# Two float32r parts for the attention scores, laid out on two halves of the partitions, in a macaron transformer block

## What is computed

```python
q = bitnet_linear(hidden_states, q_weight, q_scale)   # 32 heads of 16
k = bitnet_linear(hidden_states, k_weight, k_scale)   # 8 heads of 16
v = bitnet_linear(hidden_states, v_weight, v_scale)
...
scores = jnp.einsum('bhqd,bhkd->bhqk', q, k) / np.sqrt(HEAD_DIM)
attn = jax.nn.softmax(scores, axis=-1)
out = jnp.einsum('bhqk,bhkd->bhqd', attn, v)
```

## Time and profile before

| what | us |
|---|---|
| median of 3 runs | 1261.84 |
| span of the profiled execution, first to last instruction | 1259.9 |
| busy: TensorE matmuls (PE) | 1121.5 |
| busy: VectorE (DVE) | 935.9 |
| busy: ScalarE (ACT) | 715.8 |
| busy: GpSimd (POOL) | 276.3 |

### The profile page before, as it was taken

One profiled execution on the slowest core, in us unless ns is written; L12 is line 12 of the kernel. 1 busy time (PEld: TensorE's weight loads), 2 busy tenths in 40 slices (PEclk: granted clock), 3 DMA queues, 4 the chain that ended last, 5 costly groups with the idle time before them and its releaser, 6 DMA issues.

```text
span 1259.9 us, 20469 instructions
## 1 busy us (share of the span) xinstructions
PE 1121.5 (89%) x5944; PEld 478.0 (38%) x5944; DVE 935.9 (74%) x1855; ACT 715.8 (57%) x1313; POOL 276.3 (22%) x455
## 2 busy tenths in 40 slices
PE   1768677799999999999999999999999999998847
PEld 1556554233423342334233323333333333332335
DVE  3686867877787788887688778867886798783164
ACT  2342522365776667675567566756665676667611
POOL 3143524610330042220032003100400140022010
PEclk9998888699999999999999989999999999999979
DMA  7012132211010102100201021102001200200200
GB/s 234 17 51 82 63 95 78 69 33 38 27 56 24 41 25 80 38 25 24 75 23 33 15 78 32 30 31 68 24 24 41 57 28 24 70 11 5 78 6 34
DMA packets 87374, 59.39 MB, mean 47 GB/s; under 512 B 44144, under 2 KB 73328, under 8 KB 87280
## 3 DMA queue, kind: packets, MB, share of 16 engines
q1 hardware_dynamic: 87280, 58.39, 15.8%
HBM read 37.64 MB, written 20.32 MB: 46 GB/s over the span
## 4 chain that ended last, share of the span: by engine, by line
PE 72%; DVE 17%; issue 4%; ACT 3%; POOL 2%; DMA 1%; DVEq 0%; SPq 0%; ACTq 0%; POOLq 0%
PE ps_score L1199 18%; PE ps_out L1211 18%; PE ps_max L1186 10%; PE ps_fill L1143 7%; DVE neg_max_parts L995 6%; PE ps_fill L1186 5%; PE ps_fill L1116 2%; PE ps_fill L1170 2%; DVE neg_max_parts L1062 2%; PE ps_fill L1147 2%; PE ps_out L1219 1%; PE ps_fill L1128 1%; DVE xt_l L947 1%; DVE zm L904 1%; PE ps_fill L1160 1%
## 5 line engine op out<-in xcount | busy, mean ns | idle before, releaser
L770 ACT ACTIVATE probs<-ps_score 128x512 f32<-128x512 f32 x1024 | 567.7, 596 | 323.1 <-PE ps_score L1199 308.0
L995 DVE TENSOR_REDUCE neg_max_parts<-ps_max 128x1 f32<-128x512 f32 x630 | 417.3, 683 | 118.5 <-PE ps_max L1186 114.9
L1199 PE MATMUL ps_score<-qst,kst 99*128 99x512 bf16 x1024 | 397.4, 390 | 15.6 <-ACT probs L770 9.7
L1186 PE MATMUL ps_max<-kst,qst 96*128 96x512 bf16 x694 | 270.6, 392 | 21.1 <-DVE neg_max_parts L1062 15.8
L1211 PE MATMUL ps_out<-probs,v_ring 128*32 128x512 f32 x2048 | 277.1, 613 | 0.7 <-ACT probs L770 0.7
L995 DVE TENSOR_REDUCE neg_max_parts<-ps_fill 128x1 f32<-128x512 f32 x330 | 225.3, 683 | 53.1 <-PE ps_fill L1186 41.5
L1199 PEld LDWEIGHTS ps_score<-qst,kst 99*128 99x128 bf16 x1024 | 98.8, 97 | 386.1 <-ACT probs L770 330.5
L1186 PE MATMUL ps_fill<-kst,qst 96*128 96x512 bf16 x330 | 127.9, 388 | 3.0 <-DVE neg_max_parts L995 2.7
L330 POOL TENSOR_TENSOR wait_pad<-wait_pad 1x1 bf16<-1x1 bf16 x55 | 10.2, 186 | 450.8 <-DVE neg_max L1003 381.6
L1186 PEld LDWEIGHTS ps_max<-kst,qst 96*128 96x128 bf16 x694 | 68.3, 99 | 69.4 <-DVE neg_max_parts L1062 32.7
L1116 PE MATMUL ps_fill<-ident,xn 128*128 128x128 f32 x256 | 45.3, 306 | 54.1 <-ACT xn L719 32.5
(11 more groups left out here) (146 smaller groups left out, 1250.7 us busy)
## 6 DMA issues: line engine op xcount, KB each, us to landing
qst<-q_dram SPq DMA_DIRECT2D x192, 64.0 KB, 2.2
q_dram<-zm SPq DMA_DIRECT2D x24, 256.0 KB, 2.6
kst<-k_dram SPq DMA_DIRECT2D x192, 32.0 KB, 2.1
xc<-x SPq DMA_DIRECT2D x8, 512.0 KB, 3.7
x_dram<-xc SPq DMA_DIRECT2D x8, 512.0 KB, 3.0
xc<-x_dram SPq DMA_DIRECT2D x8, 512.0 KB, 4.1
out<-xc SPq DMA_DIRECT2D x8, 512.0 KB, 3.1
att_dram<-att SPq DMA_DIRECT2D x31, 128.0 KB, 2.0
```

What stands on the lines that cost most here:

```text
L770: act.activation(probs[:, kt % 2, j, :], ps_score[j % 2][:, :], ACT.Exp, scale=1.0 / HD ** 0.5).then_inc(probs_ready, 1)
L995: dve.tensor_reduce(neg_max_parts[:, uu % 2, t // 2, t % 2:t % 2 + 1], ps_max[b][:, :], AX, ALU.max, negate=True).then_inc(max_read, 1)
L1186: pe.matmul(ps_max[bnk][:, :], qst[0:SR, r, j, q * P:(q + 1) * P], kst[0:SR, r, half * 512:half * 512 + 512], start=True, stop=True).then_ ...
L1199: pe.matmul(ps_score[j % 2][:, :], kst[0:SR + PARTS, uu, kt * P:(kt + 1) * P], qst[0:SR + PARTS, uu, j, :], start=True, stop=True).then_in ...
```

## The change

`PARTS` goes from 3 to 2 and `PAIRS` from 6 to 3, and the parts are float32r instead of bfloat16. A unit's three pairs stand on 48 partitions. They are loaded twice: partitions 0 to 47, with the three rows of the maximum on 48 to 50, for the scores; and partitions 64 to 111 for the maximum. Both copies have a ring of two units and semaphores of their own. Steps S2 and S3 are gone. Every position of the plans stays as it was.

By the program, the tile of `score` (51 rows from partition 0) is then 64 x 128 at row 0, and that of `max_matmul` (48 rows from partition 64) is 64 x 128 at row 64.

```diff
-PARTS = 3
-PAIRS = 6
+RING = 2
+PARTS = 2
+PAIRS = 3
 SR = PAIRS * HD
-Q_PARTS = (0, 0, 0, 1, 1, 2)
-K_PARTS = (0, 1, 2, 0, 1, 0)
+TOP = P // 2
+SHIFTS = 3
+Q_PARTS = (0, 0, 1)
+K_PARTS = (0, 1, 0)
+LOADS = 2 * PAIRS * 16
...
-    "S0", "S1", "", "S2", "S3", "", "ST", "", "")]
+    "S0", "", "S1", "", "", "", "ST", "", "")]
...
-        qst = sb("qst", [P, UB, REP, BLK], BF16)
-        kst = sb("kst", [P, UB, S], BF16)
+        qst = sb("qst", [P, RING, REP, BLK], F32R)
+        kst = sb("kst", [P, RING, S], F32R)
...
-                if not isinstance(i, int) or UB * i + uu >= UB:
-                    sp.wait_ge(scores_ready, i * (32 * UB) + 32 * (uu - 3))
...
+            def load_for_scores(i, uu):
+
+                if not isinstance(i, int) or UB * i + uu >= RING:
+                    sp.wait_ge(scores_ready, i * (32 * UB) + 32 * (uu - RING + 1))
+                load_qk(i, uu, 0, score_loaded)
+
+            def load_for_max(i, uu):
+
+                if not isinstance(i, int) or UB * i + uu >= RING:
+                    sp.wait_ge(max_scores, tiles_done(i, uu - RING))
+                load_qk(i, uu, TOP, max_loaded)
...
+                    if kt == 0 and not (last and uu == 3):
+                        load_for_scores(i, uu + 1)
                     if kt == 0 and not (last and uu >= 1):
-                        load_qk(i, uu + 3)
+                        load_for_max(i, uu + 3)
...
-                    for v in range(3):
-                        load_qk(0, v)
+                    sp.wait_ge(const_ready, 12)
+                    load_for_max(0, 0)
+                    load_for_max(0, 1)
+                    load_for_scores(0, 0)
...
                     load_rows(0, 0, max_use(0, -1, SHIFT_POS))
+                    load_for_max(0, 2)
...
-                if pos in ("S1", "S3") and not ch.on_dve("split"):
...
+                if pos == "S1":
+                    gp.wait_ge(part_cast[s], n + 1)
+                    gp.tensor_tensor(parts[s][:, 1, :], zd[s][:, CH:CH + KQ], parts[s][:, 0, :].bitcast(F32),
+                                     ALU.subtract).then_inc(part_rest[s], 1)
...
-                if pos == "S2":
-                    act.wait_ge(part_rest[s], n * 2 + 1)
-                    act.activation(parts[s][:, 1, :], zd[s][:, CH:CH + KQ], ACT.Copy).then_inc(part_cast[s], 1)
...
-                pe.matmul(ps_max[bnk][:, :], qst[0:SR, r, j, q * P:(q + 1) * P], kst[0:SR, r, half * 512:half * 512 + 512],
-                          start=True, stop=True).then_inc(max_scores, 1)
+                pe.matmul(ps_max[bnk][:, :], qst[TOP:TOP + SR, r, j, q * P:(q + 1) * P],
+                          kst[TOP:TOP + SR, r, half * 512:half * 512 + 512], start=True, stop=True).then_inc(max_scores, 1)
...
-                pe.matmul(ps_score[j % 2][:, :], kst[0:SR + PARTS, uu, kt * P:(kt + 1) * P],
-                          qst[0:SR + PARTS, uu, j, :], start=True, stop=True).then_inc(scores_ready, 1)
+                pe.matmul(ps_score[j % 2][:, :], kst[0:SR + SHIFTS, uu % RING, kt * P:(kt + 1) * P],
+                          qst[0:SR + SHIFTS, uu % RING, j, :], start=True, stop=True).then_inc(scores_ready, 1)
...
                     if kt == 0 and has_max:
-                        pe.wait_ge(qk_loaded[(uu + 2) % UB], i * 192 + 192 * ((uu + 2) // UB + 1))
+                        pe.wait_ge(max_loaded[uu % RING], i * (UB // RING * LOADS) + LOADS * ((uu + 2) // RING + 1))
                     if kt == 0:
-                        pe.wait_ge(rows_loaded[uu], i * 48 + 48)
+                        pe.wait_ge(score_loaded[uu % RING], i * (UB // RING * LOADS) + LOADS * (uu // RING + 1))
```

More of the change, by code:

```diff
@@ L238, in macaron @@
         zneg = [t[:, ZW:2 * ZW] for t in zm]
[L240 removed]
+        parts = [t[:, 0:PARTS * KQ].bitcast(F32R).rearrange("p (c n) -> p c n", c=PARTS) for t in zm]
         raw_wb, raw_q = probs[:, 0, :, :], probs[:, 1, :, :]
@@ L245, in macaron @@
         raw_o = zm[1][:, 0:DC * D].rearrange("p (c n) -> p c n", c=DC)
[L246 to L249, removed]
+        raw_k, raw_v, raw_a = [v_all[:, i * DC:(i + 1) * DC, :] for i in range(3)]
+        raw_b = v_all[:, 3 * DC:4 * DC, :].rearrange("p c n -> p (c n)")
+        raw_vn, raw_kn = o_sb[:, 0, :], o_sb[:, 1, :]
         def bank(name):
@@ L271, in macaron @@
         scale_step = sem("scale_step")
-        qk_loaded = [sem(f"qk_loaded{r}") for r in range(UB)]
-        rows_loaded = [sem(f"rows_loaded{r}") for r in range(UB)]
+        score_loaded = [sem(f"score_loaded{r}") for r in range(RING)]
+        max_loaded = [sem(f"max_loaded{r}") for r in range(RING)]
+        rows_loaded = [sem(f"rows_loaded{r}") for r in range(RING)]
         max_scores = sem("max_scores")
@@ L352, in shift_use, with tiles_done @@
             return max_use(i, uu, 0 if last and uu >= 2 else SHIFT_POS)
+        def tiles_done(i, uu):
+            if isinstance(i, int) and UB * i + uu < 2:
+                return (32, START_USES)[UB * i + uu]
+            return max_use(i, uu - 2, 32) + 1
         def start_uses(step):
@@ L456, in load_qk @@
                 for slot in range(PAIRS):
-                    rows = slice(slot * HD, (slot + 1) * HD)
-                    sp.dma_start(qst[rows, r, :, :],
+                    rows = slice(base + slot * HD, base + (slot + 1) * HD)
+                    sp.dma_start(qst[rows, r, :, :].bitcast(F32),
                                  q_dram[Q_PARTS[slot], bass.ds(o0, REP * HD), bass.ds(t0, BLK)]
[L460 to L463, removed]
+                                 .rearrange("(j d) t -> d j t", j=REP)).then_inc(loaded[r], 16)
@@ new lines, in load_qk @@
+                    sp.dma_start(kst[rows, r, :].bitcast(F32),
+                                 k_dram[K_PARTS[slot], bass.ds((j % 2) * (UB * HD) + (uu % UB) * HD, HD), bass.ds(k0, S)]
+                                 ).then_inc(loaded[r], 16)
+            def load_for_scores(i, uu):
[6 more added lines that the diff above has]
+                load_qk(i, uu, TOP, max_loaded)
@@ L465, in load_rows @@
             def load_rows(i, uu, use):
-                r = uu % UB
+                r = uu % RING
                 sp.wait_ge(max_read, use + 1)
-                for part in range(PARTS):
-                    sp.dma_start(qst[SR + part:SR + part + 1, r, :, :].rearrange("c j (q p) -> c (j q) p", p=P),
-                                 shift_rows[REP * QT * part:REP * QT * (part + 1), uu % 2, :]
+                for part in range(SHIFTS):
+                    sp.dma_start(qst[SR + part:SR + part + 1, r, :, :].bitcast(F32).rearrange("c j (q p) -> c (j q) p", p=P),
+                                 shift_rows[REP * QT * part:REP * QT * (part + 1), uu % 2, :].bitcast(F32)
```

46 lines of the change are left out of this document (16 added, 30 removed).

## The result

The changed kernel takes 1316.73 us (median of 4 runs, 1314.83 to 1318.28) against 1261.97 in the same session: a ratio of 1.0431, 95% interval 1.0417 to 1.0446. It is 4.3% slower; I had forecast 1220, and the result is outside my range (up to 1298).

What follows compares the result with a forecast made beforehand. TensorE was taken as the bound, with slots without filler held by a loop through ACT. Slots -33 and split -9 gave -42 us, so 1261.84 became 1220, range 1203 to 1298.

Steps and rivals of the forecast that it cites:

- Pairs side by side: Score and maximum tiles on separate row halves stream together; the second adds 0.02 us, with 0.23 as the other bound.
- The plain slot: Attention slot without filler, starting at T: the loop through ACT holds it, 3.10 us becomes 3.17, +0.07 each.
- I take 0: Changing between whole-array filler and half-tile pairs costs nothing; other end 0.09 of gap plus 0.10 of open load.
- RT's row: Earlier trace of RT, a float32r filler matmul on one column tile: next score follows without gap, read as a free change.
- -33 us for the slots: All 32 attention slots of a body sum to -4.15 us, times 8 bodies.
- The first rival: Each tile change drains with its load exposed, 0.19 us at each filler end: +4.4 a body, 1288 us, chance 0.26.
- slots with both places: Four slots a body with filler in first and second place: forecast sum -2.64 us.
- first-place slots: Eight slots a body with filler in the first place only: forecast -0.12 us each, sum -0.96; draining changes +2.08.
- second-place slots: Five slots a body with filler in the second place only: forecast sum -1.60 us; with draining changes -1.23.
- Turns and transposes: Output turns and maximum transposes in slots without counted filler: +0.07 us per slot; draining changes added +2.28 a body.
- The split: Dropping a cast and a subtraction per chunk gains 9 us, mostly DVE time before attention; ends 0 and -15.
- Loads at nothing: Operand loads per unit growing from 0.58 to 1.15 MB cost nothing, being covered at a DMA share of 0.15.

Runs made afterwards that it cites:

- split_before: Kernel before the change without S2 and S3, the third part being a second copy of part two: 1252.71 us, against 1261.14 in the same session.
- move_after: Changed kernel with the filler of the first place in a slot moved behind the slot's last pair: 1254.30 us (one run).
- tail_pairs: Changed kernel with a spare maximum tile, never read, beside each score tile of the last two units of attention: 1307.85 us.
- start_pairs: Changed kernel with a spare score tile, never read, beside the maximum tiles ahead of attention, from the ninth on: 1329.94 us.

## Why the prediction was wrong

- **Pairs side by side: right.** Those of scores 2 and 3 start within 0.01, in all 32 slots of the third body; those of scores 0 and 1, where they wait, mostly 0.08 or 0.09 apart.
- **The plain slot: right.** 3.17; score 0 of the next slot came at T + 1.18 (I said 1.19), score 1 at T + 1.67, as worked out.
- **"I take 0" for the change of tile: wrong, and the first error.** It cost 0.2 each way: 0.10 of gap, 0.10 of open load. From RT's row I concluded that a float32r tile changes free. It did so for a column tile before. After the change RT has a gap too: its last matmul, at 578.78, streams 0.12, and the next pair starts at 578.98. The ends of my price, 0 and 0.19, were right: the measured price is the upper end. The forecast had -33 us for the slots; the units that have the upper clock nearly throughout took some 6 more than split_before's. That is some 39 of the 97 us between 1220 and the result.
- **The first rival: right in kind, too high in sum.** It said 5.00 for the nine-filler slot, and it takes 5.01. Its +4.4 a body came out as +0.4 in the third, or +1.4 without slot 31. It had +0.20 for the slots with both places, and they gave +0.28; +1.82 for the seven first-place slots, which took 1.22; -1.23 for the second-place slots, which gave 1.05.
- **Turns and transposes: half missed.** The turns of the output are float32 on the whole array ahead of a pair: 0.10 more than a plain slot, where the forecast had no more and the rival 0.19. The transposes of the maximum (bfloat16, whole array, between two pairs), for which the rival had 0.38 each, cost nothing: the next score waits for its exponential anyway, and their slots changed by +0.01, +0.03 and -0.04.
- **The clock: no term at all, and the larger error.** I put the clock at nothing without a reason: I read 0.98 in one window of attention and never asked what half-array tiles would do to it. It is worth 1312.8 - 1206.5 / 0.961 = 57 us by the mean clocks; 4 come back by the rest of the change, so the span grew by 53. The places where the clock is low took 56 more than in split_before. No case of mine had it, so the result lies above the price of the right rival (1288).
- **The split: right** (-9.1 against 1261.84 by itself, one run; -8.4 within its session).
- **Loads at nothing: right.** q loads land after 4.6 us instead of 2.2, and slots 0 and 8 of the third body, the first of their units, are only 0.01 and 0.03 longer.

A window answers to the earlier trace rows; PE is less busy than before because the open gaps are not counted, and all that DVE and ACT do is thinner:

```profile
940.00:1040.00 100.00, 91.79 (x509) 38.15 (x501) 75.41 (x146) 59.78 (x112) 8.82 (x27) 0.97 0.36 57
```

DVE's share fell from 79.5 to 75.4. I had said that it would rise above 80, which was tied to the gain that did not come.

What stays open: why the clock does not recover ahead of attention when a partner tile is there; what starts the low stretch of 37.5 us in the last two units, which three other kernels with single half tiles lack; and how much of the 9 us that the tiles add in the first units of the bodies is due to the half tile and how much to the changes. Both kernels stall there at the turn of the loop, and the change stays low for 7 to 10 us behind it where before it was 3 to 7.

## What to carry to other kernels

Put a row for the clock among the rows of a forecast, at every stage, and ask of each edit whether it leaves part of the array unused or breaks the stream (both went with a low clock here, neither every time); a full row of busy PE says nothing of it. When tiles of two shapes are mixed, count the changes and group the work by shape before the tiles are made smaller: moving some filler to another place was worth 62 us here (one run), more than the change cost. Compare a forecast with a run that has one of its terms alone: split_before showed that slot 31's gain belonged to no tile. Price an open load by operand type: here a float32r stationary operand behind a change or a wait cost 0.10 and a bfloat16 one nothing.

## What was not expected of the hardware

- PE's records at 200.00 busy of 200.00 us under a granted clock of 0.50 throughout, where all score and maximum tiles used half of the rows one at a time.
- More matmuls in less time: 183 in 35 us with spare tiles at 1.00, 99 without at 0.50; and at the same place other kernels with single half tiles held 1.00.
- A second half tile beside the first is all but free: from score 2 to score 3 it takes 0.33 with partners in the plain slots of the change, and 0.33 to 0.34 without any in the last units of move_after.
- The same instructions at the same place sometimes get a stretch of 13.7 us at 1.2 GHz and sometimes none (slots 26 to 28 of a body in tail_pairs and start_pairs): worth 5.5 us each time.
